# A graph layer and a mixture of experts on one core: the routing steps reordered, small loads moved, ten extra matmuls

## What is computed

```python
x = x + gnn(layernorm(x), edges, W1, b1, W2, b2)      # x: 2500 x 512, 80000 edges
xt = layernorm(x)
gate = softmax(xt @ Wg)                               # 2500 x 8
topv, topi = top_k(gate, 2)
topv = topv / (sum(topv) + 1e-6)
for e in range(8):
    h = gelu(xt @ W1[e] + b1[e])                      # 512 -> 256
    ye = h @ W2[e] + b2[e]                            # 256 -> 512
    out = out + ye * scores[:, e:e + 1]
x = x + out
```

## Time and profile before

| What | Value |
|---|---|
| Time, median of three runs | 612.76 us (612.75 to 614.2) |
| The profiled execution: its own time | 617.6 us |
| Its span, first to last instruction | 615.8 us |
| Mean granted TensorE clock | 0.953 of full speed |
| PE busy | 536.2 us, 87% of the span |
| DVE busy | 454.3 us, 74% |
| ACT, POOL busy | 281.2 us and 282.7 us, 46% each |

### The profile page before, as it was taken

One profiled execution on the slowest core, in us unless ns is written; L12 is line 12 of the kernel. 1 busy time (PEld: TensorE's weight loads), 2 busy tenths in 40 slices (PEclk: granted clock), 3 DMA queues, 4 the chain that ended last, 5 costly groups with the idle time before them and its releaser, 6 DMA issues.

```text
span 615.8 us, 13934 instructions
## 1 busy us (share of the span) xinstructions
PE 536.2 (87%) x4754; PEld 398.4 (65%) x4755; DVE 454.3 (74%) x984; ACT 281.2 (46%) x540; POOL 282.7 (46%) x240
## 2 busy tenths in 40 slices
PE   5998898999899989999999999814889999989980
PEld 3798787566476557667666565713677777767760
DVE  4989999773699998998994441896886666666672
ACT  3675686341523452335324003542565555555561
POOL 7472232020444473235324524325477676666643
PEclk9999999997899999999999999856999999999995
DMA  8347001100413431433212226936977787877765
GB/s 260 127 117 223 18 2 62 19 2 1 127 45 101 140 103 66 135 120 103 98 55 87 63 88 161 373 114 194 285 136 139 136 142 135 139 138 133 140 98 68
DMA packets 40215, 72.25 MB, mean 117 GB/s; under 512 B 12555, under 2 KB 16785, under 8 KB 39617
## 3 DMA queue, kind: packets, MB, share of 16 engines
q0 software_dynamic: 11840, 26.06, 23.2%
q1 hardware_dynamic: 21635, 32.36, 16.9%
q10 hardware_dynamic: 6680, 13.06, 6.4%
HBM read 43.97 MB, written 29.06 MB: 119 GB/s over the span
## 4 chain that ended last, share of the span: by engine, by line
PE 63%; DVE 20%; issue 6%; ACT 4%; DMA 3%; another core or an unknown queue 1%; ACTq 0%; POOLq 0%; POOL 0%; DVEq 0%; SPq 0%; PEldq 0%
PE psum L1572 23%; PE psum L1716 8%; PE psum L1726 8%; PE psum L1611 8%; PE psum L1556 5%; PE psum L1486 5%; DVE hot_lo L1158 4%; PE psum L1693 3%; DVE hot_key L1158 3%; DMA bound_rows<-in_dst,chunk_i 2%; DMA dst_i<-in_dst 1%; ACT he L922 1%; DVE xT_lo L1370 1%; DVE he_hi L1409 1%
## 5 line engine op out<-in xcount | busy, mean ns | idle before, releaser
L739 ACT ACTIVATE counts<-psum 128x400 bf16<-128x400 f32 x125 | 61.6, 507 | 129.3 <-PE psum L1556 127.9
L1572 PE MATMUL psum<-counts,z_hi 125*128 125x500 bf16 x400 | 103.4, 380 | 2.8 <-ACT h L766 1.9
L1572 PE MATMUL psum<-counts,z_lo 125*128 125x500 bf16 x400 | 102.4, 379 | 0.0
L1158 DVE TENSOR_TENSOR hot_lo<-iota_lo,lo_w 128x1024 f16<-128x1024 f16 x125 | 101.4, 811 | 0.0
L1158 DVE TENSOR_TENSOR hot_key<-iota_key,key_w 128x800 f16<-128x800 f16 x125 | 78.8, 630 | 29.7 <-PE psum L1556 29.0
L678 POOL DMA_INDIRECT out_x<-y,target_i x47 | 75.0, 1596 | 54.8 <-DVE y L1419 27.3
L922 ACT ACTIVATE he<-psum,eb_col,up_undo 128x128 f32<-128x128 f32 x94 | 42.3, 456 | 69.6 <-PE psum L1716 54.5
L1556 PEld LDWEIGHTS psum<-hot_key,hot_lo 128*128 128x128 f16 x1000 | 55.9, 98 | 26.1 <-issue 4.3
L640 POOL TENSOR_TENSOR xt<-xt_whole,xt 125x512 f16<-125x512 f32 x20 | 47.8, 2392 | 54.2 <-DVE xt L1198 40.6
L1572 PEld LDWEIGHTS psum<-counts,z_lo 125*128 125x128 f16 x400 | 39.5, 99 | 46.4 <-issue 2.3
L1716 PE MATMUL psum<-xT_hi,w_both 128*128 128x128 f16 x704 | 64.3, 220 | 5.5 <-DVE xT_lo L1370 5.5
(11 more groups left out here) (274 smaller groups left out, 1120.0 us busy)
## 6 DMA issues: line engine op xcount, KB each, us to landing
out_x<-x SPq DMA_DIRECT2D x20, 224.0 KB
xt_d<-xt SPq DMA_DIRECT2D x20, 224.0 KB
x_res<-in_x SPq DMA_DIRECT2D x19, 224.0 KB
up_raw<-in_L_ffn_W ACTq DMA_DIRECT2D x8, 512.0 KB, 4.0
up_d<-up_split ACTq DMA_DIRECT2D x8, 512.0 KB
w_both<-up_d SPq DMA_DIRECT2D x8, 512.0 KB, 7.9
w_raw<-in_L_ffn_W SPq DMA_DIRECT2D x8, 512.0 KB, 9.0
W_raw<-in_L_gnn_W ACTq DMA_DIRECT2D x2, 1024.0 KB, 5.2
```

Of the source, the lines that this page charges most:

```text
L739: act.activation(counts[:, it % 2, :, place:place + W], psum[:, WIN + w % 2, 0:MW].rearrange("p (w h) -> p h w", w=W), ACT.Copy).then_inc( ...
L1158: ins = dve.tensor_tensor(hot[:, w % RING].rearrange("p s (n two) -> p s n two", two=2), iota[:].rearrange("p (o n two) -> p o n two", o=1 ...
L1572: ins = mm(psum[:, AGG + c, 0:GN], half[:, t, c * 128:(c + 1) * 128], counts[0:P, g % 2, t], start=(t == 0 and n == 0), stop=(t == T - 1 a ...
```

## The change

On ACT and PE:

```diff
 # ACT
-            act.wait_ge(S["slots_known"], BLOCKS)
-            act.wait_ge(S["slots_known"], SCORES)
+            act.wait_ge(S["routed"], BLOCKS)
...
-            scale_bias(0, expert)
             for k in range(NB):
                 ...gelu of both halves of block k...
                 turned_high(k + 1)
+                if k == 0:
+                    act.wait_ge(S["slots_known"], SCORES)
+                    scale_bias(0, expert)
 # PE
+            pe.wait_ge(S["routed"], ENDS)
+            ends = [pe.value_load(end_i[0:1, e:e + 1], min_val=1, max_val=NB) for e in range(NE)]
             for n in range(2 * T):
                 ...the 40 matmuls for token_i...
+            for n in range(WARM):
+                mm(psum[:, 3], ident16[0:P], at_row[:, n * 4:(n + 1) * 4].rearrange("p n r -> p (n r)"), start=True, stop=True)
             pe.wait_ge(S["slots_known"], TOKENS)
-            pe.wait_ge(S["slots_known"], BLOCKS)
-            ends = [pe.value_load(end_i[0:1, e:e + 1], min_val=1, max_val=NB) for e in range(NE)]
+            turn(1, 0)
             pe.wait_ge(S["slots_known"], SCORE_PARTS)
             for n in range(2 * T):
-                if n == 24:
-                    turn(1, 0)
...
                 with pe.Fori(start, NB) as k:      # the empty blocks
+                    pe.sem_inc(S["up_done"], HC)
                     pe.wait_ge(S["xT_ready"], k * 2 + 2)
-                    pe.sem_inc(S["up_done"], HC)
```

`WARM` is 10. The product of these matmuls is read by nobody. On SP (`AHEAD` is 4, `LOADED` is 5), with the biases in two halves:

```diff
             for e in range(AHEAD):
                 load_expert(e)
-            sp.dma_start(b2_all[:].rearrange(...), ...broadcast_to([128, NE * D])).then_inc(S["b2_in"], 16)
             store(G - 2, 3)
+            load_biases(0)
             store(G - 1, 0)
+            load_biases(1)
             for q in (1, 2, 3):
                 store(G - 1, q)
+            sp.wait_ge(S["mlp2_done"], T)
+            for e in range(AHEAD, LOADED):
+                load_expert(e)
...
             for k in range(AHEAD):
                 sp.wait_ge(xg_in[k], 16)
-            for e in range(AHEAD, NE):
+            for e in range(LOADED, NE):
                 load_expert(e)
```

On DVE, `end_i` is written right behind `block_base`. The four steps of `expert_i` go behind `token_part`. Two steps of the shares go: the larger of two softmax values over their sum is 1 / (1 + second), where `second_exp` is the exponential of their difference. The two `split_low` go behind `xT_lo` of block 0. `landings()` takes the three distances back in one instruction each:

```diff
-            step(dve.reciprocal(total[:], total[:]))
-            step(dve.tensor_tensor(share[:], share[:], total[:]..., ALU.mult))
-            step(dve.tensor_tensor(share_sum[:], share[:, 0], share[:, 1], ALU.add))
-            step(dve.tensor_scalar(share_sum[:], share_sum[:], 1e-6, None, ALU.add))
+            step(dve.scalar_tensor_tensor(share_sum[:], total[:], 1e-6, second_exp[:], ALU.mult, ALU.add))
+            step(dve.tensor_scalar(share_sum[:], share_sum[:], 1.0, None, ALU.add))
             step(dve.reciprocal(share_sum[:], share_sum[:]))
...
+            dve.wait_ge(S["eb_in"], 48)
+            dve.tensor_scalar(up_undo[:]...).then_inc(S["undo_ready"], 1)
+            turned_low(0)
+            step(dve.scalar_tensor_tensor(empty[:], node_at[:], 0.0, lane[:, 0:NT], ALU.is_equal, ALU.mult))
+            step(dve.tensor_tensor(target_i[:], token_f, empty[:], ALU.add))
             split_low(0)
             split_low(1)
-            turned_low(0)
...
+                dve.tensor_tensor(meets[:, 0], now(expert_f), then(expert_near[:]), ALU.not_equal)
                 step(dve.tensor_tensor(changes[:, 1:NB], expert_all[:, 1:NB], expert_all[:, 0:NB - 1], ALU.not_equal))
                 step(dve.scalar_tensor_tensor(rows_to[:, 0:NB - 1], changes[:, 1:NB], float(N), lowest[:, 1:NB], ALU.mult, ALU.max))
-                for back in range(1, NEAR + 1):
-                    ...three tensor_tensor for each distance back...
-                for n in (1, 2):
-                    for back in range(1, NEAR + 1): ...one multiplication...
-                for back in range(1, NEAR + 1): ...landed_i...
+                dve.tensor_tensor(meets[:, 1], now(rows_to), then(token_near[0:1]), ALU.subtract)
+                step(dve.tensor_tensor(meets[:, 2], then(rows_near[:]), now(lowest), ALU.subtract))
+                step(dve.tensor_tensor(meets[:, 1], meets[:, 1], meets[:, 2], ALU.min))
+                step(dve.scalar_tensor_tensor(meets[:, 0], meets[:, 1], 0.0, meets[:, 0], ALU.is_gt, ALU.mult))
+                dve.scalar_tensor_tensor(landed_i[:], meets[:, 0], 16.0, then(landed_near[:, YB - NEAR:]), ALU.mult, ALU.add)
```

96 lines of the change are left out of this document (48 added, 48 removed).

## The result

| | Before | Changed |
|---|---|---|
| Median | 616.54 us (612.75 to 620.72, 20 runs) | 612.57 us (608.51 to 618.79, 20 runs) |
| Ratio | | 0.9939, 95% interval 0.9917 to 0.9961 |
| Profiled execution | 617.6 us, span 615.8 | 613.1 us, span 611.4 |

The change takes 4.0 us off, 0.6%. Forecast was 5.5, 0.9%, and 607.3 us in all, with a range to 610.4. Of the 5.3 us by which the time was missed, 3.8 are the starting point (the three times shown, median 612.76, stood at the low end of what 20 runs give) and 1.5 the difference. The same forecast from 616.54 would have been 611.0, with a range to 614.2, and 612.57 lies inside that.

What follows compares the result with a forecast made beforehand. Routing was taken as a DVE chain and the block loop as PE-bound; gains of 6.5 us (full speed) or 4.6 us (half) gave 5.5 us, so 607.3 us from 612.76, range 604.6 to 610.4.

Steps and rivals of the forecast that it cites:

- the starting point: Time of the kernel before, from which the gain was subtracted: taken as 612.76 us.
- The gelu no longer waits for scores or bias; it comes some 0.9 us behind the start of up: ACT in block 0: gelu some 0.9 us behind up's start, where it came 2.93 behind; the bias goes behind it.
- 5.66 us for 48 matmuls at half speed: PE, 40 scores and 8 turn matmuls before the change: 0.118 us each at 1.2 GHz, against 0.061 at full speed.
- the 6.1 us: Gain at the second down and everything after it at full clock; 4.2 us at half speed.
- the full-speed case: Clock up for turn and scores: they take 2.9 us, first down 5.3 us earlier, sum 6.5 us.
- the half-speed case: Clock at half for turn and scores: they take 5.4 us, first down 3.4 us earlier, sum 4.6 us.
- the ten matmuls costing nothing: Ten 512-column matmuls on PE ahead of block 0's turn: end by 419.3, before the turn can begin, delaying nothing.
- `landings()`: DVE step on which down of block 1 waits: 2.1 us instead of 2.87, saving 0.8, all on the path.
- The last store: Store that POOL needs at 416.31: at 413.4 with the expert's 2.7 us wholly ahead, still 2.9 us early.
- Stores and biases: Biases (2 MB) and expert (1 MB) moved among the last stores: taken as zero; bound, gather 0 loses 2.3 us.
- Empty blocks and expert 4, 0.2 us each: Three empty blocks save 0.05 to 0.1 us each; expert 4's earlier load gains 0 to 1 us on first blocks.
- The loop takes it back: Rival: first blocks run while weights fill DMA, giving back 2 to 4 us; 608.5 to 611 us, chance 0.15.

Runs made afterwards that it cites:

- the fourth chip: Control runs of both kernels and two edits on another chip: kernel before 599.5 us, changed kernel 590.63 us, ratio 0.9900 (only 4 runs).
- no_warm: Changed kernel without the ten extra (warm) matmuls: 612.86 us, ratio 0.9928 against the kernel before.
- sp_as_before: Changed kernel with SP's old order, biases ahead of the last five stores and expert 4 behind the gathers: 614.38 us, ratio 0.9945.
- bias_and_landings: Kernel before with only ACT's bias of block 0 behind its gelus and the new `landings()`: 615.29 us, ratio 0.9955.
- before_again: Kernel before, unchanged, profiled once more on the fourth chip: 599.5 us, ratio 1.0042 against itself.
- loads_late: Changed kernel with SP loading the weights of experts 5 to 7 only when `landings()` is done: 615.34 us, ratio 0.9981.
- lead_five: Changed kernel with POOL gathering five blocks ahead instead of eight: 593.37 us, ratio 0.9936; again on the fourth chip 596.07 us, 0.9971.
- gather_first: Changed kernel with the gather of block k + 8 ahead of the addition of block k: 590.05 us, ratio 0.989; again 593.46 us, 0.9897.
- six_late: Changed kernel with six of eight gathers behind block 0's second gelu, SP waiting for two gathers, not four: 616.19 us, ratio 0.9964.
- split_first: Changed kernel with both `split_low` back ahead of `turned_low(0)`: 612.55 us, ratio 0.9915.

## Why the prediction was wrong, step by step

**The step that failed.** The time was missed first by a term that is no part of the change, the starting point (612.76 taken, 616.54 measured, 3.8 of the 5.3 us). In the mechanism, the step that failed is "The gelu no longer waits for scores or bias; it comes some 0.9 us behind the start of up". Up started at 22.56 behind the choices matmul, forecast 22.6; the gelu came 4.6 us behind it, not 0.9, since PE's message was held. With it went the gains of the downs: counted from `token_i`, the first down came 1.7 us earlier instead of 5.3 and the second 2.5 instead of 6.1. On the chip without the hold the gelu is 1.0 us behind up, and the downs stand at 24.52 and 28.84, forecast 24.4 and 28.7. So the order of the work was read rightly and the missing thing is one delay that the forecast had at nothing.

**It could have been seen.** The forecast took 5.66 us for 48 matmuls at half speed, "0.118 us each, its message included". PE's own row gave 2.10 us for the first 24 of them, 0.088 each, and all 48 end at 426.66, 4.23 us after their start. The message comes at 428.06: 1.4 us of the 5.66 were a hold, which I put down to the clock. It too came 1.1 us behind the end of the last gather (426.93), like those of the changed kernel. On the fourth chip the same message comes within 0.1 us of the last row's end (424.93), and the 48 take 3.7 us; the other 0.5 us are the clock, which rose earlier there. The last 16 in the two profiles of the kernel before, first the one shown ahead, then the one from the fourth chip:

```profile
425.17 1.49 PE L1703 MATMUL psum<-token_part,at_row 125*128 125x96 f16 x16
```

```profile
423.97 0.96 PE L1703 MATMUL psum<-token_part,at_row 125*128 125x96 f16 x16
```

Because of this hold the 6.1 us compared a held kernel before with a changed kernel without hold. Without it in both, the second down gains 18.64 - 14.70 = 3.9 us from `token_i`; with it in both, 20.55 - 18.05 = 2.5.

**The clock.** The ten matmuls started at 410.73 and the granted clock rose to 2.4 GHz in the window 413 to 414 (0.92); it stayed there, so scores and turn took 2.3 us: the full-speed case. But the half-speed case was priced too high, at 5.4 us. On the fourth chip the clock was at 1.2 GHz again (0.50) when the turn began, and turn and scores took 3.8 us (4.0 in `no_warm`):

```profile
417.00:418.00 1.00, 1.00 (x16) 1.00 (x14) 0.93 (x3) 0.00 (x0) 0.79 (x1) 0.50 0.66 197
```

Up started at 22.55 all the same. At full speed PE waits 1.68 us for `w_lo` there; at half speed the scores matmuls end at 22.5, just behind `w_lo` (22.3). Both cases come out as one, and the difference of 1.9 us between the two sums didn't exist.

**Right as they stood.** The turn at 415.91, 18.57 behind the choices matmul, forecast 19.1; `token_part` done 18.6 behind the choices matmul, forecast 18.8; the ten matmuls costing nothing; `landings()` 426.52 to 428.62, 2.10 us, forecast 2.1, and first to second down 4.27 us instead of 5.04, 0.8 less as forecast.

**The last store, right with less to spare.** It landed 4.0 us after SP began to wait for it, at 411.0, which is 13.7 behind the choices matmul and 415.0 on the forecast's own axis: at its bound, and later than the 413.4 that it had with the expert's weights wholly ahead. POOL's first gather stood 1.3 us behind that, at 412.29, still waiting for `token_i` as before. The price of 2.7 us for the expert rested on 393 GB/s as the most that DMA moves; other windows of the same trace have more (453 from 393 to 394, 514 from 391 to 392), so that was no limit.

**Stores and biases: not zero.** The forecast asked only what the moved biases do to the last store, and there the answer, zero, held. They also stood ahead of the first of the five stores, for which DVE waits before the last tile. In the profile shown that wait is absent, in the three others with the old order (`sp_as_before`, `bias_and_landings`, `before_again`) it is 1.39, 1.82 and 1.27 us, and in none of the 16 profiles with the new order does it appear. The Trainium skill (page "DMA: Bandwidth & Descriptors", section Issuing engines are not separate DMA queues) says that DMAs run on the same 16 engines and interleave, whoever starts them. The traces agree that bytes put ahead of a store delay it, here for 2 MB by enough to make a wait of 1.27 to 1.82 us in three profiles of four; the forecast used that rule against the change, at the last store, where it was for it, at the first. The page gives no number for this.

**Empty blocks and expert 4, 0.2 us each.** The empty blocks gave what was forecast: from the second gelu of block 43, the last with rows, to the first of block 46 it is 7.02 us before and 6.74 changed, and 7.01 and 6.73 on the fourth chip, 0.3 us less in both. Of expert 4 nothing is seen: on the fourth chip the stretch from the second down to the end is 162.53 us before and 162.51 changed, with the 0.3 inside. On the chip of the result that stretch is 2.1 us longer than before, more than the 1 us that the forecast allowed. There the holds differ from one execution to the next (9.8 us of ACT's "remote" waits lie in the loop behind block 0, against 7.8 before), and once in the changed kernel, at 536 us, the clock fell to 1.2 GHz for some 3 us behind such a wait, which it never did in the loop before.

**The sum as the runs have it,** for a chip with the hold: 2.5 us at the second down, 1.3 to 1.8 us of DVE's wait in three executions of four, on average 1.1, and 0.3 of the empty blocks, some 3.9; measured 4.0. The size of the second part rests on four profiles and is argued, not shown, and since the loop itself moved by 2 us between two profiles, so close a match is partly luck. For a chip without hold 3.9 + some 1.1 + 0.3 = 5.3; measured 1.0%, 0.4 to 1.6. By time alone the two kinds of chip don't differ in what the change brings (0.9939 and 0.9900, with intervals that overlap); that they do rests on the milestones. "The loop takes it back" was the rival nearest to the outcome (0.15), but its reason, weights on DMA, is what `loads_late` excludes.

**The starting point.** The forecast noted that the profiled execution stood 4.8 us above the median of three and took the median. 17 more runs put that median 3.8 us higher.

**Open.** The hold needs a chip of one kind (the first two and the result's own against three without) and for block 0 came and went there with the number of gathers ahead of it: with eight in seven profiles, with four or two in none of three. What differs between the chips, and how a gather holds a message of PE, is not settled. On a chip with the hold, `lead_five` and `gather_first` have not run, so whether five gathers are few enough, or nine worse than eight, is open. In the loop the held blocks (ACT waits of 2 to 2.5 us) fall mostly where a gather starts 0.9 us before the last matmul of up is issued. From 440 us on a gather started 0.84 to 0.89 us ahead of it six times in the two profiles of the result, and each time up's last message came 1.9 to 2.0 us late; in the two of the fourth chip it did so nine times, and no message was late. So in the loop too it takes both, the chip and a gather at that moment. Why that moment counts was not tested.

## What to carry to other kernels

A duration taken from two rows of different engines holds the message between them too: where the engine's own rows give 0.088 us a matmul and the reader behind it 0.118, price the difference by itself, and look for waits that end "remote" before anything is built on it. When a later milestone moves, read the granted clock and every wait of that stretch before a theory gets the credit: in `sp_as_before` it was the clock, in `six_late` a landing. When transfers are moved, list every wait on what stood behind them in the queue, not only the last one, and ask whether it is absent in the profile by luck. And take the starting point from more than three runs if single executions differ by 1%.

## What the runs showed of the hardware that was not expected

- Five chips ran the same program in two groups: 616.4 to 617.5 us and 597.6 to 598.1 us. Of the 20 us between the two profiles of the kernel before, 15 lie in the block loop, 164 against 149 us from the sixth down on, and not in the granted clock, which was at full speed from 440 to 570 us in both.
- On the slower ones PE's completion messages can come up to 6 us late, several at once, while PE's issue goes on until it too stops in steps of 1.43 us. The Trainium skill (page "Perfetto Trace Analysis", section Tensor Engine Instruction (MATMUL, LD_WEIGHTS)) says that a matmul's end in a profile is estimated and the message follows after the write to PSUM is acknowledged. The trace agrees in so far as the rows end at 418.2 and the message comes at 424.2; a delay of this size is not in that page.
- Behind a hold, in which PE stood idle, the granted clock fell to 1.2 GHz (share 0.50) in `sp_as_before`, in `split_first` and once in the loop of the changed kernel; up and down then took nearly twice as long.
- Ten matmuls of 512 columns raised the clock and changed no milestone up to the second down by more than 0.06 us.
